# Attention probabilities turned by a second product of keys and queries in place of transposes

## The chip, the cores and the metric

The kernel runs on one core of a Trainium2 chip. The metric is device time in microseconds (us) of one execution. TensorE does the matrix products and transposes, VectorE and ScalarE read what it leaves in its accumulation memory (eight banks of 128 x 512 numbers), GpSimd works in the main on-chip memory only, and SyncE issues most DMAs. Each engine runs its own list of instructions in the order in which they are written; semaphores hold an instruction back until others are done.

## The reference, cut to what matters

Eight sequences of 256 tokens with 512 features go through one decoder layer. All of it is float32.

```python
x = layernorm(x + self_attention(x))        # 16 query heads of 32, 4 key/value heads, causal
x = layernorm(x + cross_attention(x, ctx))  # 16 heads of 32, causal as well
x = layernorm(x + ffn(x))                   # gates, two fused layers, four inner layer norms

def attention(q, k, v):                     # per head
    att = q @ k.T / sqrt(32)                # 256 x 256
    att = where(causal, att, -inf)
    att = softmax(att, axis=-1)
    return att @ v
```

The change lies in how `softmax(att)` and `att @ v` are computed. The feed-forward part is as it was but for the place of one addition in GpSimd's list.

## The kernel before, in words

**Precision.** Every product of float32 operands is made as three products of a rounded "high" part and a "low" remainder (`split_products`, L161). ScalarE writes the high part of what a bank holds (`hi`), and VectorE, which waits for it, the low one (`lo`, L1145). For queries and keys both parts go through a staging tile, from which DMAs of SyncE lay them in `q3` and `k3` under each other, 96 rows deep, so that one product gives all three terms of the scores.

**Turns, groups and steps.** The attention phase is a list of 16 turns of self attention (8) and cross attention (8), one for each sequence, and a short `flush`. A turn has four steps; a step takes one group of four heads. Between the attention work of a step TensorE makes "fillers": projections of queries and keys for later steps (`sq`, `sk`, `cq`, `ck`), values (`sv`, `cv`), output projections (`wo`, `wout`), transposes (`x1t`), and in the cross turns the fused feed-forward weights (`fu`). Method `fillers` is the table that says which filler stands in which step. Six of the self turns (the second to the seventh) are a hardware loop over two turns.

**The attention work of a step.** Scores of a group come in three lots: A (the first 128 queries with 128 keys, four heads), B and C (the last 128 queries with 256 keys, two heads each). For each lot TensorE makes the scores (L1442), VectorE the masked negative maxima (`maxima`, L1217), and ScalarE the exponentials with their sums over the row (`exponentials`, L1077). In the next step TensorE transposes the exponentials (L1456), 12 transposes in a group, and they are copied out of the bank to `probT` by ScalarE (lot A; in cross turns A and B) and VectorE (the rest, L1224). In the step after that, `outputs` multiplies them with the values (L1477), and two more transposes (L1481) turn the reciprocals of the row sums, which VectorE made (L1228) and GpSimd spread over 32 columns (L868). VectorE copies these out (L1234) and multiplies (L1238); GpSimd splits the result in high and low for the output projection (L844, L848).

**What sets the order.** In VectorE's list of a step stand: maxima A, reciprocals, output of the group before last, maxima B, a copy, maxima C, a copy, and then what the fillers need of it. In ScalarE's: exponentials with the copies between them, then what the fillers need. In a step with an output projection VectorE adds the result to x and takes its statistics (L1257 to L1262); GpSimd makes the inverse deviation, and VectorE normalises (L1267). GpSimd also splits the next sequence's x (`split_x`), which a DMA in ScalarE's list (L1063) brings at the start of a self turn.

The functions that the change touches follow, with the lines by which the profile names them.

## Time and profile before

| | |
|---|---|
| median of 3 runs | 918.12 us (915.69 to 924.95) |
| profiled execution | 919.1 us |
| span of its core, first to last instruction | 917.3 us |
| mean granted clock of TensorE | 0.987 of 2.4 GHz |
| busy share TensorE / VectorE / ScalarE / GpSimd | 95% / 74% / 60% / 53% |
| one turn of self attention, six of them in the loop | about 29.5 us |
| one turn of cross attention | about 41.3 us |

The span and the profiled execution's time differ by 1.8 us, which lies around the program. "Busy" of an engine is the union of its instructions' times. A duration in a row is from the start of an instruction to its end; where instructions are pipelined the next one starts earlier, so that the distance between starts is what it takes of the engine.

### The profile page before, as it was taken

How to read it: one execution, taken by the hardware profiler on the slowest of the kernel's cores; microseconds unless marked ns; L12 is line 12 of the kernel's file. 1: busy time of each engine (PE TensorE's matmuls, PEld its weight loads, DVE VectorE, ACT ScalarE, POOL GpSimd, SP SyncE). 2: the span in 40 equal slices, each digit the busy share in tenths (PEclk: the TensorE clock that was granted, in tenths of full speed). 3: DMA queues.
4: the chain of work that ended last, by engine and by line, in shares of the span. 5: the costliest groups of instructions: out<-in, count | busy, mean ns of one | idle time of the engine just before them, and what ended most of it. 6: DMA issues, size and time to landing. Idle time of an engine off the chain costs nothing.

```text
span 917.3 us, 19584 instructions
## 1 busy us (share of the span) xinstructions
PE 870.0 (95%) x5892; PEld 728.0 (79%) x5892; DVE 679.2 (74%) x2061; ACT 547.9 (60%) x1665; POOL 485.3 (53%) x792
## 2 busy tenths in 40 slices
PE   5899999999999999999999999999899999999994
PEld 5788888888887788888888887777688788778773
DVE  4688888888886977777787876857785765667556
ACT  5665556655775666565766666656635645563563
POOL 5456554664665645554645431324861672583387
PEclk9899999999999999999999999999999999999997
DMA  5654435444484956584674638533002002000001
GB/s 184 208 179 141 149 116 175 143 144 148 159 240 141 269 153 200 159 264 114 193 189 147 191 109 269 201 103 150 1 24 69 2 1 91 1 1 35 12 1 46
DMA packets 78939, 117.49 MB, mean 128 GB/s; under 512 B 7888, under 2 KB 41736, under 8 KB 78216
## 3 DMA queue, kind: packets, MB, share of 16 engines
q1 hardware_dynamic: 75416, 112.81, 39.0%
q10 hardware_dynamic: 3440, 3.67, 1.3%
q8 instruction: 40, 0.66, 0.3%
q14 instruction: 43, 0.35, 0.1%
HBM read 58.25 MB, written 17.31 MB: 82 GB/s over the span
## 4 chain that ended last, share of the span: by engine, by line
PE 45%; DVE 10%; ACT 6%; POOL 5%; issue 3%; SPq 2%; DMA 2%; DVEq 0%; POOLq 0%; ACTq 0%
PE bank L161 31%; PE bank L1456 4%; PE bank L1442 2%; PE bank L1477 2%; PE bank L1976 2%; DVE stats L1878 2%; DVE y L1885 2%; POOL rstd L1761 1%; DVE y L1923 1%; ACT ht L1832 1%; PE bank L1481 1%; POOL hT L1766 1%; POOL rstd L1759 1%; POOL xb L1772 1%; SPq L689 1%
## 5 line engine op out<-in xcount | busy, mean ns | idle before, releaser
L1077 ACT ACTIVATE prob<-bank,nmax 128x128 f32<-128x128 f32 (+1 forms) x512 | 209.2, 432 | 27.6 <-DVE nmax L1217 25.0
L161 PE MATMUL bank<-w_ffn,hT 128*128 128x512 f32 x768 | 189.0, 397 | 0.7 <-DVE hT L1643 0.7
L1217 DVE CUSTOM_DVE_ANT_0 bank<-bank,mask 128x128 f32<-128x128 f32 (+1 forms) x512 | 168.0, 386 | 2.1 <-PE bank L1442 1.6
L161 PEld LDWEIGHTS bank<-w_ffn,hT 128*128 128x128 f32 x768 | 140.3, 188 | 29.6 <-DVE hT L1643 1.9
L901 POOL TENSOR_TENSOR zone<-raw,zone 128x256 fp32r<-128x256 f32 x128 | 95.7, 779 | 59.0 <-ACT zone L1032 59.0
L1456 PE MATMUL bank<-ident,prob 128*128 128x128 f32 x768 | 120.5, 280 | 1.0 <-ACT probT L1090 0.8
L1090 ACT ACTIVATE probT<-bank 128x512 f32<-128x512 f32 x97 | 58.4, 603 | 95.3 <-PE bank L1481 93.1
L1077 ACT ACTIVATION_READ_ACCUMULATOR prob<-bank,nmax 128x1 f32 x512 | 111.6, 218 | 0.0
L1442 PE MATMUL bank<-k,q 96*128 96x128 f32 (+1 forms) x512 | 100.0, 298 | 7.8 <-DMA q<-stage 4.5
L1832 ACT ACTIVATE ht<-bank,cols 128x128 f32<-128x128 f32 x192 | 72.2, 458 | 56.5 <-PE bank L1976 56.5
L161 PE MATMUL bank<-xT,w_q 128*128 128x256 f32 x768 | 104.8, 288 | 0.6 <-DVE w_q L1137 0.6
L161 PE MATMUL bank<-zone 128*128 128x512 f32 x384 | 101.0, 400 | 2.7 <-DVE xT L1145 2.2
L161 PEld LDWEIGHTS bank<-xT,w_q 128*128 128x128 f32 x768 | 100.2, 194 | 3.9 <-DVE w_q L1137 0.8
L161 PE MATMUL bank<-w_o,oT 128*128 128x512 f32 x384 | 94.8, 396 | 3.0 <-POOL oT L848 3.0
L161 PE MATMUL bank<-xT,zone 128*128 128x512 f32 x384 | 91.7, 398 | 0.0
L1456 PEld LDWEIGHTS bank<-ident,prob 128*128 128x128 f32 x768 | 85.3, 143 | 7.1 <-issue 2.0
L161 PEld LDWEIGHTS bank<-xT,zone 128*128 128x128 f32 x384 | 72.1, 188 | 17.7 <-issue 0.5
L161 PEld LDWEIGHTS bank<-w_o,oT 128*128 128x128 f32 x384 | 70.7, 188 | 18.3 <-issue 3.6
L1442 PEld LDWEIGHTS bank<-k,q 96*128 96x128 f32 x512 | 74.7, 195 | 9.4 <-ACT prob L1077 3.6
L868 POOL TENSOR_SCALAR rwide<-rden 128x256 f32<-128x256 f32 x64 | 26.1, 409 | 104.5 <-DVE rden L1228 104.0
L161 PEld LDWEIGHTS bank<-zone 128*128 128x128 f32 x384 | 68.3, 188 | 15.9 <-DVE xT L1145 2.6
L1766 POOL TENSOR_TENSOR hT<-ht,hT 128x512 fp32r<-128x512 f32 x48 | 66.5, 1386 | 22.8 <-ACT hT L1837 22.8
(130 smaller groups left out, 1500.7 us busy)
## 6 DMA issues: line engine op xcount, KB each, us to landing
q<-stage SPq DMA_DIRECT2D x192, 128.0 KB, 2.4
k<-kstage SPq DMA_DIRECT2D x48, 256.0 KB, 4.0
x<-xres SPq DMA_DIRECT2D x16, 512.0 KB, 4.6
raw<-in_ent_wT SPq DMA_DIRECT2D x32, 256.0 KB, 4.3
raw<-in_ent_pw SPq DMA_DIRECT2D x32, 256.0 KB, 4.7
raw<-in_path_w SPq DMA_DIRECT2D x8, 512.0 KB, 3.6
xres<-in_x SPq DMA_DIRECT2D x8, 512.0 KB, 3.8
x1b<-x SPq DMA_DIRECT2D x8, 512.0 KB, 5.1
```

What stands on the lines that cost most here:

```text
L161: ins = t.matmul(out, lhs(a, k), rhs(b, k), start=first and n == 0 and m == 0, stop=last and n == len(kts) - 1 and m == 2, skip_group_chec ...
L868: g.tensor_scalar(rwide[:, i % 2, :, :].rearrange("p t (j d) -> p t j d", j=HG), src, 1.0, 1.0, ALU.mult, ALU.mult).then_inc(s_wide, 1)
L901: ins = g.tensor_tensor(tiles[:, row % 4, 1, z, c], raw[:, row % RR, z, c], tiles[:, row % 4, 0, z, c].bitcast(F32), ALU.subtract)
L1077: ins = s.activation(prob[:, u, c * width:(c + 1) * width], banks[u][:, c * width:(c + 1) * width], ACT.Exp, scale=-1.0, bias=nmax[:, i % ...
L1090: s.activation(out, src, ACT.Copy).then_inc(s_cp[u], 1)
L1217: ins = v.tensor_tensor_reduce(scored, scored, mask[:, S - width:S], scale=-1.0, scalar=3e38, op0=ALU.add, op1=ALU.min, accum_out=nmax[:, ...
L1442: ins = t_.matmul(bank[:, c * width:(c + 1) * width], qh[:, j, at:at + P], kh[:, j, 0:width], start=c == 0, stop=c == len(heads) - 1, skip ...
L1456: ins = t_.transpose(bank[:, c * P:(c + 1) * P], prob[:, u, c * P:(c + 1) * P], ident[:, :])
L1477: t_.matmul(bank[HD * j:HD * (j + 1), kt * P:S], v_, probT[:, j, kt * S:S + kt * P], start=kt == 0, stop=kt == 1, skip_group_check=True)
L1766: g.tensor_tensor(hT[:, 1, :, i * P:(i + 1) * P], ht[:, u % HT, :, :], hT[:, 0, :, i * P:(i + 1) * P].bitcast(F32), ALU.subtract).then_inc ...
L1832: ins = s.activation(ht[:, u % HT, c, :], bank[:, c * P:(c + 1) * P], ACT.Identity, bias=shift(u // BT, c), scale=gain(u // BT, c))
L1878: v.bn_stats(stats[:, i, :], y[:, i, :]).then_inc(s_bn, 1)
```

## The change

The transposes of the exponentials are gone. Each group's scores are made a second time with keys and queries exchanged, which gives them turned, and the softmax is finished inside the exponent: with the row maximum m and the row sum s, a probability is exp(score - (m + ln s)). The term -(m + ln s) enters the product as two more rows: `q3` gets the high and low part of m + ln s of each query in rows 96 and 97, `k3` holds -1 there. ScalarE's exponential of a bank is then `probT` itself. So:

- ScalarE still makes the first exponentials (for the sums), then the logarithm of the sums and its negative exponential; VectorE makes m + ln s out of them with one step of correction, in five small operations on 128 x 8 (`sums`).
- TensorE transposes the 16 columns of them (`turn_logarithms`), VectorE copies 16 x 128 out of the bank (`row_copy`), and SyncE's DMA lays them into `q3` (`load_rows`).
- Two steps behind its scores a group's turned scores are made in three lots (`turned_scores`); ScalarE's `probabilities` takes their exponentials, 512 wide each; GpSimd zeroes what the mask forbids (`masked`, two operations on 128 x 4 x 128), since the turned product isn't masked.
- The output needs no scaling: the reciprocals, their spreading, their two transposes and VectorE's multiplication are gone. VectorE writes high and low part of the output itself.
- Values of the self turns are made feature-major (12 products of 256 columns in place of 24 of 128) and turned by two transposes (`vt`).
- The score banks are two (lot C takes A's bank), the banks for fillers three. The table of fillers has marks: at `MID` TensorE makes the turned logarithms, turned lot C and score lot C, at `OUT` the outputs.

VectorE's list between two steps of the loop, in a step whose filler is a key projection (`kstage`) and a value copy (to `cv`), before the change with the same key projection:

```order
L1217 ISA bank,nmax<-bank,mask 128x256 [waits s_S]
L1217 ISA nmax 128x1
L1217 ISA bank,nmax<-bank,mask 128x256
L1217 ISA nmax 128x1
L1224 COPY probT<-bank 128x2x256 [waits s_T]
L419 REGISTER_ALU
L1145 SCALAR_TENSOR_TENSOR stage<-bank,stage 128x256 [waits s1_hi]
L419 REGISTER_ALU
L1145 SCALAR_TENSOR_TENSOR kstage<-bank,kstage 128x256 [waits s1_hi]
L152 REGISTER_ALU
L1217 ISA bank,nmax<-bank,mask 128x128 [waits s_S]
```

And with the change (L1173 is `lo`, L1278 and L1280 the output, L1258 to L1266 `sums`, L1250 the maxima):

```order
L1173 SCALAR_TENSOR_TENSOR kstage<-bank,kstage 128x256 [waits s1_hi]
L402 REGISTER_ALU
L1198 COPY cv<-bank 128x256 [waits s1_full0]
L1278 CAST oT<-bank 128x256 [waits s1_drained0,s_O]
L1280 TENSOR_TENSOR oT<-bank,oT 128x256 [waits s_oh]
...
L1258 TENSOR_TENSOR logs<-lden,nmax 128x8 [waits s_lden]
...
L1260 TENSOR_TENSOR logs<-den,logs 128x8 [waits s_lden]
...
L1262 SCALAR_TENSOR_TENSOR logs<-logs 128x8 [waits s_lse]
...
L1264 CAST logs<-logs 128x2x4 [waits s_lse]
...
L1266 TENSOR_TENSOR logs<-logs 128x2x4 [waits s_lse]
L152 REGISTER_ALU
L1250 ISA bank,nmax<-bank,mask 128x128 [waits s_S]
```

The output and the five operations of `sums` now stand between the low part of the filler and the next step's maxima A.

ScalarE's list of the same step, with the change (L1086 is `exponentials`, L1106 `probabilities`, L996 `hi`):

```order
L1086 ACTIVATE prob,den<-bank,nmax 128x128 [waits s_max]
L1086 ACTIVATE prob,den<-bank,nmax 128x128 x3
L1082 REGISTER_ALU
L1086 ACTIVATE prob,den<-bank,nmax 128x256 [waits s_max]
L1086 ACTIVATE prob,den<-bank,nmax 128x256
L1098 REGISTER_ALU
L1106 ACTIVATE probT<-bank 128x4x128 [waits s_T]
L1082 REGISTER_ALU
L1086 ACTIVATE prob,den<-bank,nmax 128x256 [waits s_max]
L1086 ACTIVATE prob,den<-bank,nmax 128x256
L1093 ACTIVATE lden<-den 128x8 [waits s_exp]
L1095 ACTIVATE logs<-lden 128x8 [waits s_lden]
```

Behind these rows comes the high part of the filler (L996), for which VectorE's low part waits. Between lots B and C one exponential of 512 columns is new, and the two small ones at the end.

The core of the diff:

```diff
@@ fillers: a self turn of the loop
-            out[0] += [("sv", 0), ("sv", 1)] + ([("sq", 2)] if wo else [])
-            out[1 if after == "self" else 0] += [("sq", 3)]
-                out[1] += [("sk", 0)]
-                    out[2] += [(wo, 0)]
-                    out[3] += [(wo, 1)]
-                out[2] += [("sq", 0)]
-                out[3] += [("sq", 1)]
+            out[0] += [("sq", 2), MID, ("vt", 0), ("sq", 3), OUT]
+                out[1] += [("sk", 0), MID, ("sv", 0), OUT]
+                out[2] += [("sq", 0), MID, (wo, 0), OUT]
+                out[3] += [("sq", 1), MID, (wo, 1), OUT]
@@ GpSimd, in every step
-                    if t.turned(i):
-                        copies(i - 1)
-                    if t.closed(i):
-                        split_output(i - 2)
...
+                    if i == 0 and t.after == "self":
+                        split_x()
...
+                    if t.closed(i):
+                        masked(i - 2)
@@ ScalarE
+                    if t.closed(i):
+                        probabilities(i - 2, 0)
+                        probabilities(i - 2, 1)
+                    if t.scored(i):
+                        if t.before or i >= 2:
+                            s.wait_ge(s_lse, t.groups(i - 2, LSE))
+                        exponentials(0)
+                        exponentials(1)
+                    if t.closed(i):
+                        probabilities(i - 2, 2)
...
+                    if t.scored(i):
+                        exponentials(2)
+                        logarithms()
@@ VectorE
                 def step(i):
+                    if t.rowed(i):
+                        sums(i - 1)
+                    if t.scored(i):
+                        maxima(i, 0)
+                    if t.rowed(i):
+                        row_copy(i - 1)
+                    if t.scored(i):
+                        maxima(i, 1)
+                        maxima(i, 2)
...
+                        elif name == OUT:
+                            output(i - 2)
@@ TensorE
                 def scores(i, u, kh, qh):
-                    bank = banks[u]
-                    if t.turned(i):
-                        t_.wait_ge(s_exp, t.groups(i - 2, U, u + 1))
+                    bank = banks[BANK_OF[u]]
+                    if u == 2:
+                        t_.wait_ge(s_exp, t.groups(i - 1, U, 1))
+                    elif t.before or i > 0:
+                        t_.wait_ge(s_exp, t.groups(i - 1, U))
...
+                def turn_logarithms(i):
+                    t_.wait_ge(s_lse, t.groups(i, LSE))
+                    t_.transpose(banks[O_BANK][0:HL, S:S + P], lse_columns[i % 2], ident[:, :]).then_inc(s_R, 1)
...
+                    heads, keys, queries = (list(range(2 * u, 2 * u + 2)), slice(0, P), slice(0, S)) if u < 2 else (list(range(HG)), slice(P, S), slice(P, S))
+                    for c, j in enumerate(heads):
+                        ins = t_.matmul(bank[:, c * width:(c + 1) * width], kh[:, j, keys], qh[:, j, queries], ...)
...
                 for i in range(t.steps()):
+                    if t.closed(i) and not (t is flush and i == 1):
+                        turned_scores(i - 2, 0)
+                        turned_scores(i - 2, 1)
+                    if t.scored(i):
+                        scores(i, 0, kh, qh)
+                        scores(i, 1, kh, qh)
                     for name in t.fillers(i):
+                        if name == MID:
+                            if t.rowed(i) and t is not flush:
+                                turn_logarithms(i - 1)
+                            if t.closed(i):
+                                turned_scores(i - 2, 2)
+                            if t.scored(i):
+                                scores(i, 2, kh, qh)
+                        if name == OUT and t.closed(i):
+                            outputs(i - 2)
```

## Rows read from the trace of the kernel before

**Rows 1.** The page: busy time (share of the span) and instructions.

```profile
PE 870.0 (95%) x5892; PEld 728.0 (79%) x5892; DVE 679.2 (74%) x2061; ACT 547.9 (60%) x1665; POOL 485.3 (53%) x792
```

**Rows 2.** Stretches: length, busy (instructions) of each engine, clock, DMA share, GB/s.

```profile
165.21:194.90 29.69, 29.39 (x262) 25.81 (x261) 24.78 (x100) 17.61 (x73) 16.49 (x31) 1.00 0.44 146
...
492.47:533.80 41.33, 41.33 (x307) 35.14 (x306) 32.18 (x109) 26.08 (x88) 21.40 (x36) 1.00 0.51 149
```

**Rows 3.** Timeline, TensorE, self step: start, length, line, operation.

```profile
149.83 0.56 PE L1442 MATMUL bank<-k,q 96*128 96x128 f32 x4
150.23 0.62 PE L1456 MATMUL bank<-ident,prob 128*128 128x128 f32 x4
150.78 0.86 PE L1477 MATMUL bank<-probT,sv 128*32 128x256 f32 x16
151.57 0.44 PE L1481 MATMUL bank<-ident,rwide 128*128 128x128 f32 x2
151.76 0.49 PE L1442 MATMUL bank<-k,q 96*128 96x256 f32 x2
...
153.23 3.02 PE L161 MATMUL bank<-w_o,oT 128*128 128x512 f32 x12
```

**Rows 4.** Lines of TensorE: value products before, per form.

```profile
L161 PE MATMUL bank<-w_kv,xT 128*128 128x128 f32 x192 | 25.7, 292 | 0.6 <-DVE o L1238 0.6
```

**Rows 5.** Timeline, VectorE, the self step before the one of rows 3.

```profile
144.44 0.29 DVE L1217 CUSTOM_DVE_ANT_0 bank<-bank,mask 128x128 f32<-128x128 f32 x1
...
145.70 0.42 DVE L1234 COPY rT<-bank 128x256 f32<-128x256 f32 x1
...
146.50 0.42 DVE L1217 CUSTOM_DVE_ANT_0 bank<-bank,mask 128x256 f32<-128x256 f32 x1
...
147.22 0.69 DVE L1224 COPY probT<-bank 128x512 f32<-128x512 f32 x1
...
150.04 0.42 DVE L1145 SCALAR_TENSOR_TENSOR stage<-bank,stage 128x256 fp32r<-128x256 f32 x1 [0.81 <-ACT stage L987]
```

**Rows 6.** Timeline, ScalarE, the same step.

```profile
145.76 0.60 ACT L1090 ACTIVATE probT<-bank 128x512 f32<-128x512 f32 x1 [1.69 <-PE bank L1481]
146.25 0.36 ACT L1077 ACTIVATE prob<-bank,nmax 128x128 f32<-128x128 f32 x1
...
147.62 0.50 ACT L1077 ACTIVATE prob<-bank,nmax 128x256 f32<-128x256 f32 x1
...
148.72 0.47 ACT L1077 ACTIVATE prob<-bank,nmax 128x256 f32<-128x256 f32 x1
...
149.63 0.38 ACT L987 ACTIVATE stage<-bank 128x256 fp32r<-128x256 f32 x1
```

**Rows 7.** Lines of ScalarE, per form: count, busy, mean ns.

```profile
L1623 ACT ACTIVATE wave<-bank,cols 128x512 f32<-128x512 f32 x16 | 10.8, 678 | 29.7 <-PE bank L161 28.3 <-issue 1.3
```

**Rows 8.** Lines of VectorE, per form.

```profile
L1224 DVE COPY probT<-bank 128x512 f32<-128x512 f32 x95 | 65.2, 687 | 0.6 <-PE bank L1456 0.6
...
L1228 DVE RECIPROCAL rden<-den 128x8 f32<-128x8 f32 x64 | 12.7, 198 | 0.6 <-ACT prob L1077 0.6
...
L1170 DVE COPY sv<-bank 128x128 f32<-128x128 f32 x16 | 4.0, 283 | 2.9 <-PE bank L161 2.9
```

**Rows 9.** Timeline, GpSimd: its split of the next x.

```profile
141.87 1.51 POOL L844 TENSOR_SCALAR xT<-raw 128x256 fp32r<-128x256 f32 x4
143.46 2.79 POOL L848 TENSOR_TENSOR xT<-raw,xT 128x256 fp32r<-128x256 f32 x4
```

**Rows 10.** Lines of GpSimd: its masking form.

```profile
L835 POOL TENSOR_SCALAR_AFFINE_SELECT mask<-mask 128x128 f32<-128x128 f32 x1 | 0.3, 282 | 0.0
```

**Rows 11.** Landing times of the DMA of x issued at L1063.

```profile
DMA to landing us min/median/max: 4.1/4.2/4.3
```

**Rows 12.** An idle stretch of TensorE, and the clock behind it (stretch).

```profile
45.78 0.66 PE L1442 MATMUL bank<-k,q 96*128 96x128 f32 x4 [3.36 <-DMA q<-stage]
...
46.00:51.00 5.00, 5.00 (x41) 4.16 (x40) 4.79 (x19) 2.99 (x12) 3.62 (x6) 0.66 0.92 264
```

372 lines of the change are left out of this document (206 added, 166 removed).

## The prediction

> **What bounds the kernel now.** I read the page's busy times first: TensorE is busy 870.0 of 917.3 us, 95%, no other engine over 75% [rows 1]. Then the stretches of single turns: in a turn of the self loop TensorE is busy 29.4 of 29.7 us at full clock, in a cross turn 41.3 of 41.3, while VectorE is busy 24.8 and 32.2 [rows 2]. So the attention phase is TensorE's list, laid end to end. The timeline shows what a step of it holds: the attention work runs from 149.83 to 153.23, 3.40 us, the rest is fillers [rows 3].
>
> The same must be asked of the other engines, since they also form a ring. In one self step VectorE starts maxima A at 144.44; ScalarE's exponentials start at 146.25 and end with the high part of the filler at 149.63; VectorE makes the low part at 150.04 and another one behind it, and is at the next maxima A at about 150.9 [rows 5, 6]. This ring took 6.4 us, in a step of 6.3 us of TensorE's list. It is closed because both engines take their lists in order: maxima, exponentials, high part, low part, next maxima. What is put into it lengthens the short steps at once. That is the reader's key to the change: not what TensorE saves, but what the ring gains.
>
> **TensorE.** Removed in each of 64 groups: 12 transposes and the two of the reciprocals. The first four took 150.23 to 150.78, 0.55; the two 0.19; the four lots between 151.76 and 153.23 (two of scores, two of transposes) 0.37 each [rows 3]. That is 0.55 + 2 x 0.37 + 0.19 = 1.48 us. Added: two turned lots of two products of 256 columns (0.37 each, as such a score lot), one of four of 128 columns (0.40, as 149.83 to 150.23), and one transpose of 16 columns, bounded by 0.10 (half of the 0.19 for two) and 0.19; I take 0.15. Sum 1.29, so 0.2 us less in a group. The values of a self turn: 24 products cost 25.7 us in all 8 turns, 3.2 a turn [rows 4]; 12 of 256 columns cost half of the 3.02 us of 12 output products of 512 columns [rows 3], 1.5, and two transposes 0.19: 1.5 less. TensorE's sum is -0.2 x 64 - 1.5 x 8 = -25 us, if it stays the bound.
>
> **The ring of a self step after the change.** First the ring of before without what the new order takes out. ScalarE's copy and its wait for TensorE (145.76 to 146.25, and some 0.2 before) leave the way between maxima A and exponentials: -0.7. The step with a key projection has one filler of this kind and not two: -0.4. Lot C's exponentials waited 0.2 for their maxima; the new exponential before them covers that. 6.4 - 1.3 = 5.1 us. Then what is put in, from the order shown with the change:
>
> - turned lot C's exponential, 512 columns, between lots B and C. The copy of 512 took 0.60 [rows 6], the nearest activation with a table 0.68 [rows 7]. I take 0.68; ends 0.60 and 0.75 (0.34 for 128 columns in lot A [rows 6] and more for each further 128).
> - logarithm and negative exponential of 128 x 8, the second waiting for the first, before the filler's high part. No such row; the nearest is lot A's pace of 0.34 for 128 columns, from below half of that. I take 0.3 each: 0.6, ends 0.4 and 0.9.
> - a copy of values, which stands behind the low part: 0.4.
> - the output, two operations on 128 x 256 out of a bank, which now stands behind the low part: 145.70 to 146.50, 0.8 [rows 5].
> - `sums`, five operations on 128 x 8 in a chain. The reciprocal of this size took 0.198 [rows 8]. Five of 0.2 and the waits between them: 1.2; from below 0.5 (half the reciprocal each), from above 1.75 (0.15 for each wait).
>
> Together 3.7: this step goes from 6.4 to 8.8 us, while TensorE has 6 us of work for it. By the Trainium skill (Perfetto Trace Analysis, Optimizing Scalar/DVE Operations) a VectorE instruction on the main memory has about 60 ns of overhead and shows about twice that in a profile. By that estimate `sums` would be 0.6 and the whole kernel some 36 us faster than my sum; the reciprocal's 198 ns is above it, and I stay with the row.
>
> **A whole turn** I count on VectorE, since in this ring it is either busy or waits for ScalarE. Its busy time of a self turn was 24.8 [rows 2]. Per step it gains `sums` 1.2 and the row copy 0.28 (as the 128-column copy), and loses the reciprocal 0.20 and two copies of 0.687 [rows 8]: -0.1. The value copies add 0.2 a turn. So 24.6. In each step it waits while ScalarE goes from exponentials A to the filler's high part: 150.04 - 146.25 = 3.8, less the 0.2 of lot C, plus 0.68 and 0.6: 4.9. In this time it has the row copy (0.2) and maxima B and C (0.72 each, 146.50 to 147.22 [rows 5]): 3.3 are idle. 24.6 + 4 x 3.3 = 37.8; the waits inside chains and for the deviation, which now stand before the next maxima, add 1.1. **Self turn: 38.9 in place of 29.5 us, +9.4; six of them +56.** First and last self turn have the same ring with parts missing or wider fillers: +6 each.
>
> **Cross turn:** 32.2 busy [rows 2], +0.6 a step (here one copy leaves, not two), 4 x 3.3 idle, 0.8 in chains: 48.6 in place of 41.3. Unit additions that need nothing of ScalarE fill some of the idle time, and products that now come late (TensorE holds score lot C until exponentials A are done, since they share a bank, and all behind it) open as much again; I let these cancel. **+7.3, for seven turns +51.** Last cross turn and flush: the last group's turned products and exponentials stand before the gates: +5. The feed-forward part, about 297 us, stays: one addition in GpSimd's list moves, and GpSimd waits there anyway.
>
> Costed at nothing: the row DMA (8 KB). It has from the middle of a step to the next step's start, about 4.5 us, for an issue and a landing; q's DMAs are larger and its cover is the ring itself. GpSimd's masks: one 128 x 128 took 0.282 [rows 10]; four times as wide I take 0.75 (ends 0.4, with a pace below the fixed part, and 1.13). They stand between ScalarE and TensorE's outputs, not in the ring. SyncE has one issue more in a step and now waits for turned lot C before it overwrites `q3`; the projections concerned are needed two steps later.
>
> **Sum:** 919.1 (the profiled execution) + 56 + 12 + 51 + 5 = 1043 us; the median of the runs is 1.0 below the profiled one: 1042. TensorE would be busy about 80% of it.
>
> **Rivals.**
>
> *It gains: 893 us.* TensorE remains the bound and its 25 us come off. For it: it is 95% busy, and every filler was moved so that ScalarE's and VectorE's work lies two steps back. The condition is a ring under TensorE's 27.1 us a self turn (29.4 less 0.2 x 4 and 1.5), 6.8 a step. Against it: the ring without the logarithms, `sums` and value copy is 5.1 + 0.68 + 0.8 = 6.6 already, and two of four steps add an output projection with its statistics to VectorE. It would need those parts in the shadow, which the order excludes. 5%; another 2% that gain and stalls cancel, 905 to 930.
>
> *GpSimd's list decides, 964 us.* At the head of a self turn it now splits the next x before it masks. The DMA of x lands 4.2 us after its issue [rows 11], the split takes 4.4 (141.87 to 146.25 [rows 9]), two masks 1.5: TensorE could not make its outputs before 10 us in a turn, its step 0 would last 10.9 and the others about 7.9 (masks and outputs behind turned lot C): 34.6, +5.1 x 6 = 31, and +2 in a cross turn (14). This shows alone only if the ring is shorter than I say, for the ring puts the outputs of that step as late. 7%.
>
> *The clock falls, 1065 us and more.* After 3.36 us without work, TensorE's next 5 us ran at a granted 0.66, in part at 1.2 GHz, and lost 1.7 us [rows 12]. In the new ring it waits up to 3 us in one piece, in the steps with an output projection. 60 such stretches would cost 100 us if TensorE bound; in a ring that waits for others I take a quarter of that. [...] 8%.
>
> *The ring as computed* has the rest, 78%. Its ends: with all cheap bounds 1.0 us less in each of some 60 steps, 983; with all dear ones 0.8 more, 1090.
>
> **The numbers.** Predicted 1042. The range is the ring's own, opened below for steps that hide more than I see: 970 to 1090. It leaves out the two gains and the GpSimd case (14%) and the worst of the clock. What a measurement here can tell from no change is 1%. Faster 5%, same 2%, slower 93%.
>
> **What the profile after would show.** VectorE busy nearly as before in a turn, with idle pieces of 3 us whose releaser is ScalarE's high part or the maxima's way back; TensorE idle before score lot C (waiting for exponentials A) and before the outputs; self turns near 39 us. The five operations of `sums` at 1.2 us from first to last, the 512-wide exponentials at 0.68. If TensorE is still over 93% busy, I am wrong in the ring; if the waits before the outputs name GpSimd and step 0 of a self turn alone is long, the second rival is right; if the clock is under 0.95 in the loop, the third. Wrong in size it would be if the small operations cost half or double.

## The result

| | before | after |
|---|---|---|
| median | 917.75 us (915.69 to 924.95, 4 runs) | 1170.86 us (1169.99 to 1178.34, 4 runs) |
| ratio of the two, 95% interval | | 1.274 (1.266 to 1.283) |
| span of the profiled core | 917.3 us | 1176.6 us |
| mean granted clock | 0.987 | 0.883 |

The changed kernel is 27% slower. The forecast was 1042, range 970 to 1090: the direction was right, the size 129 us too small. The profiled execution of after, 1178.3 us, is 7 us over its median, so the spans differ by 259 us where the medians differ by 253.

Which stages hold it? A turn is measured here from one turn's first reciprocal (before) or row copy (after) to the next turn's, which stand at about the same place of a step. I give the mean of the stage. The feed-forward part starts with the first product of `w_ffn`.

| stage | before | forecast | after |
|---|---|---|---|
| up to the first mark | 49.1 | 55.1 | 63.6 |
| six self turns, each | 29.8 | 39.2 | 44.7 |
| last self turn | 33.8 | 39.8 | 52.0 |
| first cross turn | 49.0 | 56.3 | 71.4 |
| six cross turns, each | 41.6 | 48.9 | 56.6 |
| last cross turn and flush | 59.9 | 64.9 | 85.7 |
| feed-forward part | 297.1 | 297.1 | 295.9 |

So it is missing everywhere in the attention phase, 5.5 us in a self turn of the loop and 7.7 in one of the six cross turns. The four single stages at the ends and in the middle are missed by more, 8.5, 12.2, 15.1 and 20.8 us, together 57 of the 136 us that the attention phase took over its forecast in this execution; no experiment below looks at them alone. The feed-forward part is as forecast. Within a self turn of the loop, by the distances between row copies, the four steps took 9.8, 9.5, 11.9 and 13.6 us on average: it is the last two, with an output projection, that are long.

### The profile page after: what moved, and what is told of

Same layout as the page of the kernel before. It is cut to its first block, busy times and chain, and to the rows that moved or that the text cites. A ratio compares the mean times of both kernels' runs of the same rounds, so it can differ in the third digit from the quotient of the medians.

```text
span 1176.6 us, 19282 instructions
## 1 busy us (share of the span) xinstructions
PE 943.5 (80%) x5492; PEld 762.2 (65%) x5492; DVE 743.1 (63%) x2286; ACT 622.6 (53%) x1888; POOL 472.9 (40%) x729
## 4 chain that ended last, share of the span: by engine, by line
PE 39%; DVE 28%; ACT 16%; issue 9%; POOL 5%; DMA 2%; DVEq 0%; SPq 0%; ACTq 0%; POOLq 0%
PE bank L161 30%; ACT prob L1086 9%; DVE bank L1250 4%; PE bank L1497 4%; DVE logs L1264 2%; DVE nmax L1250 2%; PE bank L2058 2%; DVE logs L1262 2%; PE bank L1546 2%; DVE stats L1960 1%; DVE oT L1278 1%; DVE stats L1302 1%; DVE xres L1299 1%; DVE logs L1258 1%; DVE y L2005 1%
## 5 line engine op out<-in xcount | busy, mean ns | idle before, releaser
L1086 ACT ACTIVATE prob<-bank,nmax 128x128 f32<-128x128 f32 (+1 forms) x512 | 208.5, 422 | 225.6 <-DVE nmax L1250 225.3
L1250 DVE CUSTOM_DVE_ANT_0 bank<-bank,mask 128x128 f32<-128x128 f32 (+1 forms) x512 | 169.6, 380 | 105.6 <-PE bank L1497 102.7
L161 PE MATMUL bank<-w_ffn,hT 128*128 128x512 f32 x768 | 190.4, 399 | 5.9 <-DVE w_ffn L1747 3.7
L1497 PE MATMUL bank<-k,q 96*128 96x128 f32 (+1 forms) x512 | 99.4, 321 | 108.4 <-ACT prob L1086 107.3
L1106 ACT ACTIVATE probT<-bank 128x512 f32<-128x512 f32 x192 | 109.1, 604 | 115.7 <-PE bank L1524 111.9
L161 PEld LDWEIGHTS bank<-w_ffn,hT 128*128 128x128 f32 x768 | 141.4, 190 | 35.7 <-issue 4.5
L1497 PEld LDWEIGHTS bank<-k,q 96*128 96x128 f32 x512 | 77.9, 216 | 117.7 <-ACT prob L1086 116.4
L877 POOL TENSOR_SCALAR_AFFINE_SELECT probT<-probT 128x512 f32<-128x512 f32 x64 | 41.2, 644 | 259.8 <-ACT probT L1106 259.8
L161 PE MATMUL bank<-w_o,oT 128*128 128x512 f32 x384 | 129.2, 503 | 0.0
L161 PE MATMUL bank<-xT,w_q 128*128 128x256 f32 x768 | 122.8, 319 | 2.2 <-DVE w_q L1165 1.9
L161 PEld LDWEIGHTS bank<-xT,w_q 128*128 128x128 f32 x768 | 117.3, 228 | 4.5 <-DVE w_q L1165 2.4
L161 PE MATMUL bank<-zone 128*128 128x512 f32 x384 | 108.4, 426 | 8.2 <-DVE kstage L1173 5.2
L1524 PE MATMUL bank<-q,k 98*128 98x256 f32 (+1 forms) x512 | 95.9, 314 | 20.0 <-DMA q<-log_rows 8.4
L161 PEld LDWEIGHTS bank<-w_o,oT 128*128 128x128 f32 x384 | 96.7, 259 | 22.7 <-issue 0.3
L1086 ACT ACTIVATION_READ_ACCUMULATOR prob<-bank,nmax 128x1 f32 x512 | 105.4, 206 | 0.0
L1524 PEld LDWEIGHTS bank<-q,k 98*128 98x128 f32 x512 | 75.1, 208 | 33.8 <-issue 31.7
L161 PE MATMUL bank<-xT,zone 128*128 128x512 f32 x384 | 94.7, 406 | 0.0
L161 PEld LDWEIGHTS bank<-zone 128*128 128x128 f32 x384 | 75.8, 207 | 25.2 <-DVE kstage L1173 7.1
L161 PEld LDWEIGHTS bank<-xT,zone 128*128 128x128 f32 x384 | 74.5, 195 | 18.1 <-issue 0.2
L874 POOL TENSOR_SCALAR_AFFINE_SELECT probT<-probT 128x512 f32<-128x512 f32 x64 | 41.1, 642 | 99.5 <-ACT probT L1106 99.4
```

What stands on the lines that cost most here:

```text
L161: ins = t.matmul(out, lhs(a, k), rhs(b, k), start=first and n == 0 and m == 0, stop=last and n == len(kts) - 1 and m == 2, skip_group_chec ...
L874: g.affine_select(out=probT[:, :, 0:P], in_=probT[:, :, 0:P], compare_op=ALU.is_ge, fill=0.0, base=0, pattern=[[0, HG], [1, P]], channel_m ...
L877: g.affine_select(out=probT[:, :, S:PW], in_=probT[:, :, S:PW], compare_op=ALU.is_ge, fill=0.0, base=0, pattern=[[0, HG], [1, P]], channel ...
L1086: ins = s.activation(prob[:, u, c * width:(c + 1) * width], banks[BANK_OF[u]][:, c * width:(c + 1) * width], ACT.Exp, scale=-1.0, bias=nma ...
L1106: s.activation(out, src, ACT.Exp).then_inc(s_cp[u], 1)
L1250: ins = v.tensor_tensor_reduce(scored, scored, mask[:, S - width:S], scale=-1.0, scalar=3e38, op0=ALU.add, op1=ALU.min, accum_out=nmax[:, ...
```

## The profile after

The page's line of busy times, which answers to [rows 1]:

```profile
PE 943.5 (80%) x5492; PEld 762.2 (65%) x5492; DVE 743.1 (63%) x2286; ACT 622.6 (53%) x1888; POOL 472.9 (40%) x729
```

No engine is the bound any more. TensorE has 400 instructions less and is busy 73 us *longer*: its products take longer. Stretches of a self turn of 41.3 us and a cross turn, as [rows 2], and 45 us of the loop:

```profile
289.70:331.01 41.31, 30.36 (x231) 24.96 (x232) 26.53 (x112) 23.11 (x89) 13.93 (x23) 0.92 0.31 104
684.06:738.61 54.55, 46.51 (x285) 37.69 (x286) 37.60 (x132) 30.07 (x98) 19.13 (x30) 0.87 0.42 127
191.00:236.00 45.00, 33.77 (x233) 27.68 (x232) 27.13 (x112) 24.47 (x96) 15.30 (x27) 0.81 0.29 97
```

The granted clock is 0.81 to 0.92 of 2.4 GHz, so part of each stretch ran at 1.2. What TensorE waits for (total, times, longest):

```profile
PE bank L1497 <- ACT prob L1086: 107.3, 61, 3.3
PE bank L1504 <- DVE logs L1266: 50.2, 39, 5.0
PE bank L1546 <- POOL probT L877: 13.0, 15, 1.7
PE bank L1524 <- DMA q<-log_rows: 8.4, 1, 8.4
```

The largest is score lot C (L1497), waiting in nearly every step for the exponentials of lot A (L1086), whose bank it takes. The next is the transpose of the logarithms, waiting for the last operation of `sums`. How a step goes, in the timeline of a self step with an output projection (TensorE, VectorE, ScalarE and GpSimd; it answers to [rows 3, 5, 6]):

```profile
308.02 0.64 DVE L1266 TENSOR_TENSOR logs<-logs 128x8 fp32r<-128x8 f32 x1
308.59 0.28 DVE L1250 CUSTOM_DVE_ANT_0 bank<-bank,mask 128x128 f32<-128x128 f32 x1
...
309.71 0.37 ACT L1086 ACTIVATE prob<-bank,nmax 128x128 f32<-128x128 f32 x1 [3.42 <-DVE nmax L1250]
...
311.27 0.80 PE L1497 MATMUL bank<-k,q 96*128 96x256 f32 x2 [1.87 <-ACT prob L1086]
...
311.86 4.02 PE L161 MATMUL bank<-w_o,oT 128*128 128x512 f32 x12
...
312.26 0.43 DVE L1250 CUSTOM_DVE_ANT_0 bank<-bank,mask 128x256 f32<-128x256 f32 x1 [1.67 <-PE bank L1497]
...
314.97 0.42 DVE L1173 SCALAR_TENSOR_TENSOR stage<-bank,stage 128x256 fp32r<-128x256 f32 x1 [1.84 <-ACT stage L996]
...
315.81 0.86 PE L1546 MATMUL bank<-probT,sv 128*32 128x256 f32 x16
316.01 0.69 DVE L1299 TENSOR_TENSOR xres<-bank,xres 128x512 f32<-128x512 f32 x1 [0.61 <-PE bank L161]
...
317.67 0.39 DVE L1278 CAST oT<-bank 128x256 fp32r<-128x256 f32 x1
...
318.44 0.15 DVE L1258 TENSOR_TENSOR logs<-lden,nmax 128x8 f32<-128x8 f32 x1
...
318.79 0.63 POOL L874 TENSOR_SCALAR_AFFINE_SELECT probT<-probT 128x512 f32<-128x512 f32 x1
318.90 0.54 DVE L1264 CAST logs<-logs 128x8 fp32r<-128x8 f32 x1
...
320.08 0.30 DVE L1250 CUSTOM_DVE_ANT_0 bank<-bank,mask 128x128 f32<-128x128 f32 x1 [0.43 <-issue]
```

Follow it from maxima A (308.59) to maxima A (320.08), 11.5 us: exponentials A, score lot C, the twelve products of the output projection (311.86 to 315.88, 4.0 us), addition to x, statistics, output, `sums`. From 311.27 to 315.88 this chain runs through TensorE. The forecast's ring did not: it went from the exponentials straight to the filler's high part. That way is nearly as long here: VectorE's low part ends at 315.39, and the addition waits 0.61 us more, for the products. And it runs through lot C as well, since maxima C (312.26) had waited 1.67 us for it.

## The experiments

Each kernel is the changed kernel or the kernel before with the edit shown; times are medians, each timed beside runs of the kernel before on the same chip.

**The third score bank.** Lot C in a bank of its own; the fillers have two.

```diff
-P_BANKS = (2, 3, 4)
+P_BANKS = (3, 4)
-S_BANKS = (0, 1)
-BANK_OF = (0, 1, 0)
+S_BANKS = (0, 1, 2)
+BANK_OF = (0, 1, 2)
-                    if u == 2:
-                        t_.wait_ge(s_exp, t.groups(i - 1, U, 1))
-                    elif t.before or i > 0:
-                        t_.wait_ge(s_exp, t.groups(i - 1, U))
+                    if t.before or i > 0:
+                        t_.wait_ge(s_exp, t.groups(i - 2, U, u + 1))
```

> The changed kernel, with a third bank for scores: score lot C has a bank of its own again, so TensorE makes it without waiting for the exponentials of lot A; the banks for fillers are two. In the changed kernel TensorE waited 107 us in 61 places before score lot C. Theory A (the ring runs through TensorE: lot C waits for the exponentials A, and all fillers behind lot C come late, so that their high and low parts, which stand before the next maxima A, come late too): these waits go, and the time falls by 40 to 90 us, to 1080 to 1130, most of it in cross turns (from about 55 us) and in steps with an output projection. Theory B (the ring is VectorE's and ScalarE's lists alone, as predicted): the waits move to other places of TensorE's list; only the 0.3 to 0.5 us by which lot C's exponentials came late go, 1140 to 1160. Theory C (the lower granted clock decides): as the waits do not get less, under 10 us of gain.

Measured: 1159.7 us, ratio to before 1.262 (1.259 to 1.266). The 107 us of waits are gone, the time is not. Its waits of TensorE:

```profile
PE bank L1545 <- POOL probT L878: 51.5, 30, 3.9
PE bank L1503 <- DVE logs L1267: 44.1, 29, 7.0
PE bank L161 <- DVE stage L1174: 38.1, 17, 5.3
PE bank L161 <- DVE kstage L1174: 27.1, 7, 4.4
```

Fillers (L161) now wait for a bank that VectorE has not emptied, and the outputs' wait for GpSimd has grown from 13.0 to 51.5 us. In the self turns of the loop the steps with an output projection became shorter, 9.8 and 12.2 us in place of 11.9 and 13.6, and step 0 longer, 12.6 in place of 9.8. By itself this looks like theory B; the last pair of experiments shows that it isn't.

**Fewer operations in `sums`.** Two in place of five.

```diff
-                    v.tensor_tensor(less_max[k], ...)
-                    v.tensor_tensor(ratio[k], ...)
-                    v.scalar_tensor_tensor(lse[k], ...)
-                    v.tensor_copy(lse_parts[k][:, 0, :, :], lse[k])
-                    v.tensor_tensor(lse_parts[k][:, 1, :, :], lse[k], ...)
+                    v.tensor_tensor(lse_parts[k][:, 0, :, :], lden[:, k, :, :], nmax[:, k, :, :], ALU.subtract)
+                    v.tensor_tensor(lse_parts[k][:, 1, :, :], lden[:, k, :, :], lden[:, k, :, :], ALU.subtract)
```

> The changed kernel with `sums` cut from five operations in a chain to two without one (ln of the sum minus the negative maximum is written as if it were rounded, the low part is zero; what is left out is the correction step and the low part). It takes some 0.9 to 1.3 us out of VectorE's list in each of 63 steps. Theory B (ring of VectorE and ScalarE): it comes off in full, 55 to 80 us, 1090 to 1115. Theory A (ring through TensorE) says the same, since `sums` stands before maxima A in either ring. If TensorE or its clock set the time: under 20 us.

Measured: 1077.5 us, ratio 1.172 (1.167 to 1.177): 93 us less. From the first operation to the end of the last, `sums` took 106 us in the changed kernel (64 times 1.66) and takes 28 here, so 78 us of work gave 93. It lies on the ring in full. The 15 us more are not explained by it; the granted clock rose with it, from 0.883 to 0.925, and TensorE's waits for lot C fell from 107.3 to 69.1 us.

**Products in TensorE's wait,** in every step, and then only in steps 2 and 3 of the turns, where an output projection can follow:

```diff
+                    if u == 2 and t.own:
+                        for _ in range(12):
+                            t_.matmul(bank[:, 0:P], ident[:, :], ident[:, :], start=True, stop=True, skip_group_check=True)
@@ the second form
+                    if u == 2 and t.own and t.before and i >= 0:
```

> The changed kernel with 12 products of 128 columns of the identity more before turned lot C of each group (overwritten by it): about 1.3 us of work at the full clock in each of some 61 steps, at the place where TensorE waited 1.7 us on average for the exponentials A. Theory C (the waits lower the granted clock, and the output projections, 4.5 us in place of 2.9, lie on the ring): the granted clock rises from 0.88 to 0.95 and more, the twelve products of an output projection take 3 us, and the time falls by 30 to 60 us, to 1110 to 1140. Theories A and B without C: the work fills a wait in the short steps and lengthens the others: 1170 to 1200.

Measured: 1189.8 us, ratio 1.294 (1.290 to 1.298), granted clock 0.953: most of the clock is back, and the kernel is 19 us slower, so that what was added lies on the ring, at least in part.

> The changed kernel with the 12 products of the identity before turned lot C only in the steps in which an output projection follows (and the other two of each second half of a turn, 30 steps). With them in all steps the granted clock rose from 0.88 to 0.95, the output projection took 2.98 us again in place of 4.1, and yet the time rose by 19 us. If the slow output projections lie on the ring (theory C), and the 1.3 us of dummies fit in TensorE's wait: 1.1 us less in each of 30 steps, about 1140, the other 30 steps as in the changed kernel. If they do not lie on it, or if the dummies delay score lot C by as much as they give back: 1165 to 1180.

Measured: 1160.4 us, ratio 1.262 (1.258 to 1.266), clock 0.923. The 384 products of the output projections in the changed kernel, and in this one (busy, mean ns):

```profile
L161 PE MATMUL bank<-w_o,oT 128*128 128x512 f32 x384 | 129.2, 503 | 0.0
```

```profile
L161 PE MATMUL bank<-w_o,oT 128*128 128x512 f32 x384 | 95.2, 398 | 0.0
```

Before it was 94.8. The low clock costs 34 us in these products. 10 us came back, after what the added products cost, and how much that is no run shows. The trace of the changed kernel gives an estimate from above for this place. For each of the 32 output projections I take the smaller of two times: what it took over the 2.97 us of before, and how long VectorE's addition waited for it. Together they are 28 us. So the clock's part is 10 us or more, and in these products at most about 28.

**GpSimd's masks** cut to 2 of 128 columns.

```diff
-  g.affine_select(out=probT[:, :, 0:P], in_=probT[:, :, 0:P], ..., pattern=[[0, HG], [1, P]], ...)
+  g.affine_select(out=probT[:, :, 0:2], in_=probT[:, :, 0:2], ..., pattern=[[0, HG], [1, 2]], ...)
```

> The changed kernel with GpSimd's two masking operations cut to 2 of 128 columns (the rest of the turned probabilities is left unmasked). Theory D (an operation of VectorE that touches the main memory only is held while GpSimd runs one: the rounding operation of `sums`, L1264, took 0.54 us in the median, the others of this size 0.16): L1264 falls to 0.17, the ring gets 0.35 us shorter in 63 steps, and the 13 us for which TensorE's outputs waited on GpSimd go: 1170 - 22 - 13, about 1135. Without D: L1264 stays at 0.54, and the time falls by 0 to 13 us, 1157 to 1170.

Measured: 1153.6 us, ratio 1.257 (1.252 to 1.262): 17 us less, between the two forecasts. The rounding operation of `sums` in the changed kernel and here (ns, min/median/max):

```profile
L1264 DVE CAST logs<-logs x64: 171/543/3261, 29.1 to 846.0; 128x8 fp32r<-128x8 f32 x64
```

```profile
L1264 DVE CAST logs<-logs x64: 171/172/671, 29.1 to 817.7; 128x8 fp32r<-128x8 f32 x64
```

`sums` as a whole fell from 106 to 88 us, 18, which is the 17 of the time. The mechanism of theory D is there, and its size was missed: the rounding fell from 0.47 to 0.31 us on average, since GpSimd's other work still holds `sums` (1.38 us on average, where five operations that nothing holds take 0.85).

**`sums` in VectorE's idle time.**

```diff
-                        sums(i - 1)
                         maxima(i, 0)
-                        row_copy(i - 1)
                         maxima(i, 1)
+                        sums(i - 1)
                         maxima(i, 2)
+                        row_copy(i - 1)
@@ TensorE at MID
-                                turn_logarithms(i - 1)
                                 turned_scores(i - 2, 2)
                                 scores(i, 2, kh, qh)
+                                turn_logarithms(i - 1)
```

> The changed kernel with `sums` behind maxima A and B in place of ahead of A, the row copy behind maxima C, and the transpose of the logarithms behind score lot C. Nothing is left out; VectorE does `sums` while it would wait for ScalarE. Theory B (the ring maxima A, exponentials, high part, low part, output, `sums`, maxima A): `sums` took 1.66 us on average from first to last, all of it on the ring; cutting it to 0.43 gave 93 us. Moved off the ring it gives 90 to 105 us: 1065 to 1080. If what counts is VectorE's total work or the chain from logarithms to the row DMA (which gets later by about 2 us), the gain is under 40 us, or the kernel is slower.

Measured: 1070.0 us, ratio 1.166 (1.161 to 1.170): 101 us less, as theory B said. With the two kernels built on it below (1070.9 and 1069.9) it is the fastest form of the change that I ran.

**The additions without the rest.** The kernel before with the 512-wide exponential, logarithm, negative exponential and `sums`:

```diff
+                        if u == 1:
+                            ins = s.activation(banks[u][:, :], banks[u][:, :], ACT.Exp, scale=0.0)
...
+                        s.activation(lden, den[:, i % 2, :, :], ACT.Ln).then_inc(s_lden, 1)
+                        s.activation(inv, lden, ACT.Exp, scale=-1.0).then_inc(s_lden, 1)
@@ VectorE, ahead of maxima A
+                        sums(i - 1)
```

> The kernel before, with what the change adds to ScalarE's and VectorE's lists and nothing else: a 512-wide exponential between lots B and C, logarithm and negative exponential of 128 x 8 behind lot C, and the five operations of `sums` ahead of the next maxima A (their results are not used; TensorE, GpSimd, SyncE and the table of fillers are as before). Theory B: the ring was 6.4 us in a step of 6.3 of TensorE's list, so what is added, 0.6 + 0.5 + 1.6 = 2.7 us, comes on in nearly every short step and in part in the long ones: 2.7 x 28 self steps + 1.5 to 2.7 x 32 cross steps, 120 to 160 us, 1040 to 1080. If VectorE and ScalarE had slack that takes it up (they were 74% and 60% busy): under 40 us, below 960.

Measured: 1010.5 us, ratio 1.099 (1.096 to 1.103): +91. Less than forecast; perhaps the steps with long fillers had slack, which no run shows. But it is far from free. The granted clock was 0.960 here, so this number too holds slower products.

**The shared bank without the rest.** The kernel before, lot C in lot A's bank:

```diff
-                    bank = banks[u]
-                    if t.turned(i):
-                        t_.wait_ge(s_exp, t.groups(i - 2, U, u + 1))
+                    bank = banks[(0, 1, 0)[u]]
+                    if u == 2:
+                        t_.wait_ge(s_exp, t.groups(i - 1, U, 1))
+                    elif t.turned(i):
+                        t_.wait_ge(s_exp, t.groups(i - 1, U))
```

VectorE and ScalarE read lot C from the same bank. Lots A and B now wait until all exponentials of the group before are done, where each had waited for its own lot.

> The kernel before with one part of the change: score lot C takes lot A's bank, so TensorE makes it only when the exponentials of lot A of the same group have read the bank; the third score bank lies idle. In the profile before, maxima A started at 144.44 and the exponentials A ended near 147.6, 3.1 us later, while TensorE came to lot C some 2 us after lot A. Theory A (sharing the bank ties TensorE's fillers to ScalarE): a wait of 1 to 1.5 us in each of some 60 steps, 60 to 90 us, 980 to 1010. If the wait is taken up by other slack of VectorE and ScalarE, or their order lets lot C come late without harm: under 20 us, below 940.

Measured: 1070.9 us, ratio 1.168 (1.163 to 1.174): **+153 from the shared bank alone.** That is far over the forecast of theory A, 60 to 90. The granted clock is 0.94, but the output projections run at full speed (2.99 us). TensorE's wait, and a step of it:

```profile
PE bank L1444 <- ACT prob L1077: 114.4, 66, 3.6
```

```profile
188.96 0.56 PE L1444 MATMUL bank<-k,q 96*128 96x128 f32 x4
...
189.98 0.29 DVE L1217 CUSTOM_DVE_ANT_0 bank<-bank,mask 128x128 f32<-128x128 f32 x1
...
191.72 0.36 ACT L1077 ACTIVATE prob<-bank,nmax 128x128 f32<-128x128 f32 x1
...
193.28 0.50 PE L1444 MATMUL bank<-k,q 96*128 96x256 f32 x2 [1.47 <-ACT prob L1077]
...
196.81 1.60 PE L161 MATMUL bank<-xT,w_q 128*128 128x256 f32 x12
...
198.44 0.38 ACT L987 ACTIVATE stage<-bank 128x256 fp32r<-128x256 f32 x1 [2.54 <-PE bank L161]
```

Lot A at 188.96, lot C only at 193.28, the fillers behind it, and the high part at 198.44, which ScalarE awaits for 2.54 us. In [rows 6] the same high part (L987) waited for nothing.

> The kernel before with the additions to ScalarE's and VectorE's lists (which alone gave 1010 us, +91) and with score lot C in lot A's bank as well. Theory A (the changed kernel's 1170 us are the additions, made worse by TensorE's wait before lot C, behind which its fillers and so the high and low parts come late): the two effects add up or more, 1070 to 1130. If the shared bank only moves a wait that TensorE has anyway once the ring is the bound (theory B): within 25 us of 1010.

Measured: 1177.8 us, ratio 1.284 (1.278 to 1.289). The two together, 260 us, are a little over their sum, 244, and as much as the whole change (253); theory A had said 1070 to 1130. This kernel still has the transposes and copies that the change takes out, so that the agreement in size may be chance; it shows that the two suffice for a loss of this size. TensorE waits 177.0 us here before lot C.

**Shorter ring behind the moved `sums`.** The output behind the next maxima A; then also the logarithms behind the high parts.

```diff
                         maxima(i, 0)
+                        output(i - 3)
...
@@ ScalarE, next kernel
-                        logarithms()
...
                             projection(t, name)
+                        logarithms()
```

> The changed kernel with `sums` behind maxima A and B (which gave 1070 us) and with the output's two operations of VectorE (0.8 us) moved from the end of a step to behind the next step's maxima A, where VectorE would wait. Theory B: the output was the last part on the way from the filler's low part to maxima A: 0.8 us in 56 to 62 steps, 45 to 50 us: 1020 to 1025. If by now TensorE's waits before score lot C or the turned scores' wait for the row DMA set the step: under 20 us of gain.

> As the kernel with the late output, and with the logarithm and its negative exponential (0.45 us of ScalarE) behind the high parts of the fillers in place of ahead of them. Theory B: 0.45 us less in some 60 steps, 25 us under the kernel with the late output. If ScalarE waits for the filler's products at that point anyway (its high parts waited 15.6 and 8.5 us for TensorE in the profiles so far): under 8 us.

Measured: 1070.9 us, ratio 1.167 (1.163 to 1.172), and 1069.9 us, 1.164 (1.160 to 1.169). Neither gives anything, where 45 to 50 us and another 25 had been expected: with `sums` moved, these parts no longer lie on what bounds.

**The branch.** Six self turns written out.

```diff
-        with eng.Fori(0, ROUNDS) as r:
-            for t in selfs:
-                t.r = r
-                body(t)
+        for t in selfs:
+            body(t)
```

> The changed kernel with the six middle self turns written out, without the hardware loop. In the changed kernel the step in which the loop branches back took 16 to 17 us in place of 11.3 (twice in the loop, and the entry and the exit have the same branch), VectorE idle for 2.3 us and its small operations 0.6 to 0.7 us each behind it. If the branch is what costs: 2 x 5 us, perhaps 4 x 3 more at entry and exit: 1150 to 1160. If the long steps come from the data (x of the next turn, q's DMAs) and only fall together with the branch: 1170 within 3.

Measured: 1160.7 us, ratio 1.261 (1.257 to 1.266): 10 us. The branch in the changed kernel, with GpSimd beside it:

```profile
149.78 0.73 DVE L1309 TENSOR_SCALAR xres<-xres,mv,rstd 128x512 f32<-128x512 f32 x1 [0.32 <-POOL rstd L899]
...
151.59 2.77 POOL L855 TENSOR_TENSOR xT<-raw,xT 128x256 fp32r<-128x256 f32 x4
152.85 0.17 DVE L1258 TENSOR_TENSOR logs<-lden,nmax 128x8 f32<-128x8 f32 x1 [2.33 <-issue]
152.97 0.73 DVE L1260 TENSOR_TENSOR logs<-den,logs 128x8 f32<-128x8 f32 x1
153.73 0.65 DVE L1262 SCALAR_TENSOR_TENSOR logs<-logs 128x8 f32<-128x8 f32 x1
154.31 0.64 POOL L874 TENSOR_SCALAR_AFFINE_SELECT probT<-probT 128x512 f32<-128x512 f32 x1
154.41 0.56 DVE L1264 CAST logs<-logs 128x8 fp32r<-128x8 f32 x1
```

VectorE is idle for 2.33 us here and for 2.95 at the loop's other branch back; without the loop both are gone. The long operations behind the idle time are another matter: they end when GpSimd's do (154.38 beside 154.36, 154.97 beside 154.95), as in turns without a branch.

**Both loops open?** Third score bank and moved `sums`; all moves together, and GpSimd's masks ahead of its split of the next x; score lot C later in TensorE's list, in the changed kernel and in the one with `sums`, output and logarithms moved:

```diff
-                out[2] += [("sq", 0), MID, (wo, 0), OUT]
-                out[3] += [("sq", 1), MID, (wo, 1), OUT]
+                out[2] += [("sq", 0), (wo, 0), MID, OUT]
+                out[3] += [("sq", 1), (wo, 1), MID, OUT]
```

> The changed kernel with two moves: third score bank (two for fillers) and `sums` behind maxima A and B. `sums` moved alone gave 1070, the third bank alone 1160. Two loops, each a bound alone: the two together give more than their sum (101 + 11), 970 to 1030. One loop: their sum at most, 1058 to 1070.

> The changed kernel with all the moves together: third score bank (two for fillers), `sums` behind maxima A and B, the output behind the next maxima A, the logarithms behind the high parts, and GpSimd's masks ahead of its split of the next x. Two loops, each a bound alone (TensorE's wait through the shared bank; the ring with `sums`): both are gone, and what is left of the ring (6.4 - 1.3 + 0.6 = 5.7 us) is under TensorE's work: 930 to 980, if two filler banks suffice. If one cause only is behind the slowdown and it was `sums` (already moved in the kernel of 1070 us): 1050 to 1070.

> The changed kernel with the place MID (turned logarithms, turned lot C, score lot C) one filler later in most steps, behind the output projection where there is one; the banks as they are. TensorE has 1.6 to 3 us more of work ahead of the wait for the exponentials A, so that the wait (107 us in 61 places) shrinks to under 40 us. If the ring with `sums` bounds by itself: 1140 to 1170, as with the third bank. If the shared bank is the one cause and the third bank's 11 us were small for want of filler banks: 1060 to 1100.

> The same later place of score lot C in the kernel with `sums`, output and logarithms moved (1070 us). Two loops: both are eased, 980 to 1030. If a later lot C makes its own maxima and exponentials late instead (they and the logarithms stand behind it): 1050 to 1100.

Measured: 1111.3 us (ratio 1.210, 1.204 to 1.216), 1110.1 (1.210, 1.204 to 1.215), 1182.4 (1.288, 1.281 to 1.296) and 1138.8 (1.237, 1.229 to 1.244). All four missed on the slow side. In the first, TensorE's transpose of the logarithms stands behind a lot C that waits for nothing, and so waits for `sums` itself:

```profile
PE bank L1503 <- DVE logs L1267: 58.4, 45, 6.4
PE bank L161 <- DVE stage L1174: 22.4, 12, 3.1
```

A later lot C makes TensorE's wait for it smaller (44.0 us) and its outputs' wait for GpSimd larger, from 13.0 to 79.0, since the turned lot C moved with it.

**Two banks for fillers, the third idle,** lot C still in A's bank, in the changed kernel and in the one with `sums` moved:

```diff
-P_BANKS = (2, 3, 4)
+P_BANKS = (3, 4)
```

> The changed kernel with two banks for fillers in place of three; the third lies idle, and score lot C is in lot A's bank as in the changed kernel. Beside the kernel with a third score bank and two for fillers (1160 us) it shows the shared bank alone. If the third filler bank is worth 50 to 100 us here, so that the shared bank costs as much as well and the 11 us were a difference of two large terms: 1220 to 1270. If filler banks are worth little, the ring with `sums` bounds and the shared bank costs little in its shadow: 1165 to 1190.

> The kernel with `sums` behind maxima A and B (1070 us), with two banks for fillers in place of three and the third idle. Beside the same with a third score bank (1111 us). If the shared bank costs what it costs in the kernel before, 100 us and more: 1210 and more. If it costs some 30 to 50 us: 1140 to 1160. If nothing: 1111, and the 41 us are the filler bank's.

Measured: 1221.6 us (ratio 1.328, 1.324 to 1.333) and 1128.2 us (1.226, 1.220 to 1.232). So the third filler bank is worth 51 us in the changed kernel (1221.6 - 1170.9), and the shared score bank costs 62 (1221.6 - 1159.7), measured where the fillers have two banks. The 11 us of the first experiment were the difference of the two. Once `sums` is moved they are 58 and 17. The clock is in the 62 as well: an output projection took 4.17 us on average with the shared bank and 3.14 without, 33 us over the 32 of them.

## Why the forecast had the direction and missed the size

**Right.** TensorE stopped being the bound (80% busy, as forecast). `sums` went on the ring (93 and 101 us), and the output stands in the chain of the timeline; that the two small activations lie on it no run shows. In the step of the key projection the forecast was 8.8 us; the distances in the loop are 8.8 to 10.1, 9.5 on average. The signs named for the profile came: TensorE idle before score lot C, waiting for exponentials A. The exponential of 512 columns takes 0.604 (0.68 taken), the mask 0.64 (0.75), logarithm and negative exponential 0.21 each, 0.45 together (0.6). The feed-forward part cost nothing, and the row DMA nothing but one wait of 8.4 us, at the end of the first cross turn.

**The step that failed** is one half sentence: "products that now come late (TensorE holds score lot C until exponentials A are done, since they share a bank, and all behind it) open as much again; I let these cancel". The wait was seen and priced at nothing net in the cross turns, and in the self turns not at all: the 1.1 us a turn there are for chains and the deviation. But with the shared bank TensorE itself is a link of the ring: lot A, maxima A, exponentials A, lot C, fillers, high part, low part, next maxima A. In the kernel before, sharing the bank costs 153 us, more than all that was put into VectorE's and ScalarE's lists (91), and both together give the loss. In the changed kernel with two filler banks it costs 62 us against the same with a third score bank, while the third filler bank, which it buys, gives 51.

**A term too small:** `sums`, 1.2 us forecast, is 1.66 on average: its operations take 0.16 each alone, but 0.3 to 0.6 where GpSimd is at work. Over 64 groups that is 29 us, and of the 1.9 us by which VectorE is busy longer in the self turn above (26.5) than forecast (24.6) it is 1.8. 17 of the 29 came back without the masks.

**A rival that was part of the truth:** the clock. I had given it 1065 and more, and a weight of 8%; its sign, under 0.95 in the loop, came true. The waits before lot C were 1.8 us on average (107.3 in 61 places), not 3, and that sufficed: an output projection took 4.0 us in place of 3.0. Its share is 10 us or more, and at most about 28 in these products, which are slower by 34. The forecast took a quarter of what the stretches cost, for a ring that waits for others; where the slow products are links of the ring, more of it counts. By the Trainium skill (TensorE: Matmul & The Clock Gate, Why this matters for your kernels), idle gaps between bursts of products are what to avoid. The trace agrees, with 0.883 for 0.987, though nearly all gaps here are shorter than those of which that section warns.

**Not seen:** the branch, 10 us.

62 + 29 + 10 + 10 are 111 of the 129 us, but they are no account of it: the 62 hold slow products as well, so that they overlap with the clock's part, and all were measured in different kernels. What is shown is that the shared bank, priced at nothing, is large; how the 129 us divide isn't settled, nor is what bounds the kernel of 1070 us, 16.6% over before. TensorE still waits 64.2 us for lot C there, and 19.0 for the row DMA, which the forecast had at nothing; the third bank doesn't help since other waits (for `sums`, for filler banks) come in its place. No form that I ran comes near the kernel before.

The rival "GpSimd's list decides" was wrong for the changed kernel (13.0 us of TensorE's waits), but it appears once the other waits are taken away: 51.5 us with the third score bank.

## What to carry to other kernels

Sharing a bank between two lots that used to have their own puts a wait for VectorE and ScalarE into the middle of TensorE's list; walk the ring again with TensorE as a link before pricing it, and ask which fillers stand behind the wait. Put short chains of small operations where their engine waits anyway, not ahead of the operation that starts the next step: moving the same five operations gave 101 us. When taking a resource back gives little, run the kernel that gives it to nobody: the 11 us were 62 less 51.

## What the runs showed of the hardware

- VectorE's small operations of `sums`, which touch the main memory only, are held while GpSimd works. In the changed kernel the cast of 128 x 8 took 0.63 us on average in the 42 cases where GpSimd was busy at its start and 0.17 in the 22 others; the other four 0.29 to 0.58 against 0.16 to 0.17. All 120 that took over 0.24 us ended within 0.04 us of the end of an operation of GpSimd. Operations that read a bank did not change (0.42 against 0.41 for `oT`). The Trainium skill (Advanced Engine Details and Errata, VectorE Performance Modes) says that the second port of VectorE to the main memory is shared with GpSimd and that instructions of VectorE that use both ports and those of GpSimd block each other; its table gives such a mode to the cast and none to operations with two input tensors. The trace shows both held.
- TensorE's clock fell without a long pause: six waits of 1.2 to 2.4 us within 45 us of the loop (191 to 236) went with a mean of 0.81, where the kernel before, without such waits, had 1.00 [rows 2].
- Behind the loop's two branches back VectorE stood idle for 2.33 and 2.95 us, without a wait that the profile shows; with the turns written out both are gone and the kernel is 10 us faster. In the kernel before the same branch cost little: from first reciprocal to first reciprocal, the two turns that end with it took 29.8 and 29.7 us, the two behind them 29.4.
